# Division, bias, residual add and store moved from a stage of their own into the last third of the attention rows (graph network kernel, one core)

## The chip, the cores and the metric

The kernel runs on one core of one Trainium2 chip. The metric is the device time of one execution in microseconds (us), the lower the better. Three executions of the kernel before gave 4484.0, 4495.23 and 4496.08 us; the median is 4495.23 us.

## What is computed

Two message-passing layers on a graph of 12500 nodes (128 features) and 200000 edges, sorted by destination. The first layer ends in `x1` (the input plus its result). The second, an attention layer with 4 heads of 32 features, is where the change lies:

```
h = relu(layernorm(x1));  hW = (h @ W).reshape(N, 4, 32)
e = leaky_relu(a_src[src] + a_dst[dst], 0.2)         # edges and self loops
p = exp(e - segment_max(e, dst)[dst])
denom = segment_sum(p, dst)
out = segment_sum(hW[src] * p, dst) / (denom + 1e-16)   # per head
result = x1 + out + bias
```

The kernel sums numerator and denominator together and divides once at the end.

## The kernel before

Nodes lie in 98 windows of 128 nodes (a node is a partition), edges in 196 blocks of 1024. The attention pass walks 294 steps; each step handles one pair of an edge block and a window that meet, and passes on to the next block or window (196 + 98 = 294). Two steps make a row of the loop; the table `steps` in SBUF holds the block and window numbers of each row, and every engine loads its numbers from it at the row's start. In a row `u` is 0 in the first step and 1 in the second. The steps are software-pipelined: at step j the engines do the front of step j, the node part of j-1, the edge part of j-2 and the sum of j-3 or j-4. The order on each engine is that in which the code is written; semaphores join the engines.

The names that the change and the prediction touch:

- `a_G`: the rows of `Htab` for a block's edges, gathered by GpSimd (line 502) into 7 slots; SyncE tells VectorE (`ready`) that a block has landed.
- `a_Sb` (line 1354, VectorE): a one-hot matrix; ScalarE casts it to `a_S32` in two halves (line 1498), the second half when TensorE is done with the old one.
- `a_csh` (line 1358, VectorE), then `a_psD` (TensorE, line 1515), then `a_tt` (line 1394, VectorE).
- `a_ST` (line 1464, ScalarE): a copy of TensorE's transposes `a_psT`, and the first thing ScalarE does in a step.
- `a_GP` (line 1448, VectorE): the gathered rows times the edge weights, the last thing VectorE does in a step. TensorE sums it into `a_psA` (line 1525), 8 matrix products of float32, shown as 16.
- `acc`, shown as `arena` (128 partitions x window x 4 heads x 33): 32 sums and the denominator of each head. ScalarE scales it (line 1477), and VectorE adds `a_psA` to it (line 1350), the first thing VectorE does in a step.

VectorE loads the numbers of its row at line 1326, between `a_GP` of the row before and line 1350.

Window w gets its last sum at step 196 + w - 1 at the latest, so from step 197 on windows become final one after another.

After the attention pass a barrier closes its block of code. `final_phase` then works on 14 groups of 7 windows: SyncE loads `x1keep` into `f_x` (line 1582) and stores `f_o` to `out` (line 1587), GpSimd adds the bias (line 1606), VectorE forms the shares 1/(denominator + 1e-16) for all windows (lines 1613 and 1615), multiplies (line 1625, 7 instructions a group) and adds `f_x` (line 1634).

Of the kernel before, what the change touches and what calls it, by code (L numbers as in the profile page):

```python
# [25 lines left out]
P = 128  # L26
N, E = 12500, 200000
D, ED, H = 128, 64, 64
NH, HC = 4, 32
# [12 lines left out]
PIECE = 14  # L42
NG = W // GW
# [7 lines left out]
assert W == NG * GW and NG % 2 == 0 and NS % 2 == 0 and NB % SLOTS == 0  # L51

# [29 lines left out]
def build(nc, t, out):  # L82

    main = ExitStack()
    with main:
# [47 lines left out]
        with ExitStack() as ctx:  # L133
            attention_pass(nc, t, k, Htab, flagrows, lambda *a: sb(*a, ctx=ctx), sem, ctx)
        with ExitStack() as ctx:
            final_phase(nc, t, k, x1keep, out, lambda *a: sb(*a, ctx=ctx), sem, ctx)
# [45 lines left out]

def group(dram, g):

    return dram.rearrange("(g w p) f -> g p w f", w=GW, p=P)[bass.ds(g, 1)].rearrange("o p w f -> p (o w) f")
# [5 lines left out]


def run_groups(eng, body):


    body(0)
    with eng.Fori(1, NG // 2) as i:
        body(i)
# [271 lines left out]
def run_pairs(eng, body, count, depth, first=None):  # L470

    def edge(j, back):
        return 0 <= j - back < count
    for row in range(3):
        body(row, edge)
        if row == 0 and first is not None:
            first()
    with eng.Fori(3, count // 2 - 1) as row:  # L480
        body(row, lambda j, back: True)
    for row in range(count // 2 - 1, (count + depth + 1) // 2):
        body(row, edge)
# [764 lines left out]
def attention_pass(nc, t, k, Htab, flagrows, sb, sem, ctx):  # L1248
# [17 lines left out]
    GP = two("GP", [P, C, HR])  # L1266
    pst = lambda name, shape, dt=F32: ctx.enter_context(nc.psum_tensor(f"a_{name}", shape, dt))
# [6 lines left out]
             "h1 r1 h2 h3 EX eq es ed ep GP ACh ACC am ag").split()  # L1274
# [4 lines left out]
    with nc.Block() as block:  # L1279
# [12 lines left out]
        def _(dve):  # L1292
# [32 lines left out]
            def body(row, live):  # L1325
# [6 lines left out]
                for u in range(2):  # L1332
# [86 lines left out]
                    if node:  # L1419
# [31 lines left out]
            run_steps(dve, body, 4)  # L1451

        @block.scalar
        def _(act):
# [45 lines left out]
            run_steps(act, body, 3)  # L1500
# [67 lines left out]
def final_phase(nc, t, k, x1keep, out, sb, sem, ctx):  # L1568

    xs = [sb(f"f_x{u}", [P, GW, D]) for u in range(2)]  # L1570
    os_ = [sb(f"f_o{u}", [P, GW, D]) for u in range(2)]
    den = sb("f_den", [P, 2, W, NH])
    s_x = [sem(f"f_slotx{u}") for u in range(2)]
    s_st = [sem(f"f_stored{u}") for u in range(2)]
    s_v, s_xb, s_m, s_o = (sem(f"f_{n}") for n in ("v", "xb", "m", "o"))
    with nc.Block() as block:
        @block.sync
        def _(sp):
            def load(g, u, done):
                if due(done):  # L1580
                    sp.wait_ge(s_o, done)
                sp.dma_start(xs[u][:, :, :], group(x1keep, g)).then_inc(s_x[u], 16)  # L1582

            def store(g, u):
                if due(g + 1):
                    sp.wait_ge(s_o, g + 1)
                sp.dma_start(group(out, g), os_[u][:, :, :]).then_inc(s_st[u], 16)  # L1587

            for u in range(2):
                load(u, u, 0)  # L1590
            with sp.Fori(0, NG // 2 - 1) as i:
                for u in range(2):
                    load(2 * i + 2 + u, u, 2 * i + u + 1)
                    store(2 * i + u, u)
            for u in range(2):
                store(NG - 2 + u, u)
            for u in range(2):
                sp.wait_ge(s_st[u], 16 * (NG // 2))

        @block.gpsimd  # L1600
        def _(pool):
            def body(i):
                for u in range(2):
                    if due(16 * (i + 1)):
                        pool.wait_ge(s_x[u], 16 * (i + 1))
                    pool.tensor_tensor(xs[u][:, :, :], xs[u][:, :, :], bc(k["gbias"][:, :], 1, GW),
                                       ALU.add).then_inc(s_xb, 1)
            run_groups(pool, body)

        @block.vector  # L1610
        def _(dve):
            link = Count()
            dve.tensor_scalar(den[:, 0], k["acc"][:, 0:W, HC:HR:HC + 1], 1e-16, None, ALU.add).then_inc(s_v, 1)  # L1613
            dve.wait_ge(s_v, link())
            dve.reciprocal(den[:, 1], den[:, 0]).then_inc(s_v, 1)  # L1615
            dve.wait_ge(s_v, link())

            def body(i):
                for u in range(2):
                    g = 2 * i + u  # L1620
                    acc, share = k["acc"][:, bass.ds(g * GW, GW), :], den[:, 1, bass.ds(g * GW, GW), :]
                    if due(16 * i):
                        dve.wait_ge(s_st[u], 16 * i)
                    for w in range(GW):
                        ins = dve.tensor_tensor(  # L1625
                            os_[u][:, w, :].rearrange("p (h c) -> p h c", c=HC),
                            acc[:, w, 0:HR].rearrange("p (h c) -> p h c", c=HC + 1)[:, :, 0:HC],
                            bc(share[:, w, :], 2, HC), ALU.mult)
                    ins.then_inc(s_m, 1)
                    if due(g + 1):  # L1630
                        dve.wait_ge(s_m, g + 1)  # L1631
                    if due(g + 1):
                        dve.wait_ge(s_xb, g + 1)  # L1633
                    dve.tensor_tensor(os_[u][:, :, :], os_[u][:, :, :], xs[u][:, :, :], ALU.add).then_inc(s_o, 1)  # L1634
            run_groups(dve, body)


# [35 lines left out]
```

## Time and profile before

| | |
|---|---|
| median of three executions | 4495.23 us (4484.0 to 4496.08) |
| the profiled execution's own time | 4484.96 us |
| its span, first to last instruction | 4483.2 us |
| rows 100 to 145 of the attention pass | 3749.6 to 4377.6 us |
| rows 146 to 148 | 4377.6 to 4403.3 us |
| last stage | 4403.3 to 4483.2 us |
| busy share of the span: TensorE, its weight loads, VectorE, ScalarE, GpSimd | 86%, 78%, 54%, 60%, 72% |
| granted TensorE clock, mean | 0.80 of full speed |

Times in rows are microseconds from the span's start. A busy share is a mean over stages that differ, so the stages are read by themselves below. "Idle" is the time in which an engine ran no instruction, with the releaser that ended it; "issue" means that the profile shows nothing that it waited for.

### The profile page before, as it was taken

The page shows a single profiled execution, that of the slowest core. Times are in us where ns is not written, and L with a number is a line of the kernel's source. Part 1 is how long each engine was busy: PE and PEld are TensorE (multiplying, and loading weights), DVE is VectorE, ACT ScalarE, POOL GpSimd, SP SyncE. Part 2 cuts the span into 40 slices and gives each one's busy share as a digit, 9 for nine tenths or more (in the row PEclk, how much of TensorE's full clock was granted, in tenths as well). Part 3 has the DMA queues.
Part 4 walks back from the last instruction along what each step waited for, and adds up shares of the span by engine and source line. Part 5 has one row for each costly group of instructions (what it writes and reads, how often), then busy time and mean ns, then how long its engine had stood idle before and what let it go on. Part 6 is the DMA issues. An engine that isn't in the chain of part 4 may idle for free. (4 is left out here: it accounts for less than half of the span.)

```text
span 4483.2 us, 130400 instructions
## 1 busy us (share of the span) xinstructions
PE 3855.5 (86%) x40200; PEld 3479.7 (78%) x40201; DVE 2408.8 (54%) x9866; ACT 2697.7 (60%) x4960; POOL 3218.0 (72%) x3234
## 2 busy tenths in 40 slices
PE   6788888888888888887766999999999999999992
PEld 4677777777777777776456998889999899999992
DVE  5742222222222222222765777777777777777776
ACT  5555655565555655564554666666666666666661
POOL 2777777777777777775557777777777777777772
PEclk9898898989989899897776677777777766766765
DMA  5322222222222222221332222222222222222223
GB/s 159 78 54 52 52 52 54 50 54 52 52 52 52 52 52 52 52 52 44 100 109 56 55 56 55 54 55 55 55 55 55 55 55 55 56 55 55 56 53 115
DMA packets 288723, 272.91 MB, mean 61 GB/s; under 512 B 132751, under 2 KB 209829, under 8 KB 288677
## 3 DMA queue, kind: packets, MB, share of 16 engines
q0 software_dynamic: 100352, 160.76, 17.0%
q1 hardware_dynamic: 181392, 108.94, 8.6%
q10 hardware_dynamic: 6932, 2.69, 0.2%
q8 instruction: 17, 0.28, 0.0%
q14 instruction: 30, 0.24, 0.0%
HBM read 242.74 MB, written 29.40 MB: 61 GB/s over the span
## 5 line engine op out<-in xcount | busy, mean ns | idle before, releaser
L502 POOL DMA_INDIRECT a_G<-Htab,a_idx x1568 | 1526.9, 974 | 495.4 <-issue 474.7
L502 POOL DMA_INDIRECT p_rows<-Btab,p_idx x1568 | 1508.5, 962 | 478.9 <-issue 477.5
L1525 PE MATMUL a_psA<-a_GP,a_S 128*128 128x132 f32 x4704 | 949.8, 382 | 1.0 <-DVE a_GP L1448 1.0
L1525 PEld LDWEIGHTS a_psA<-a_GP,a_S 128*128 128x128 f32 x4704 | 871.7, 282 | 7.2 <-DVE a_GP L1448 1.3
L802 DVE TENSOR_TENSOR p_z<-p_psZ,p_rows 128x512 f32<-128x512 f32 x294 | 198.2, 689 | 1168.7 <-SPq L614 1124.3
L1498 ACT CAST a_S<-a_Sb 128x512 f32<-128x512 bf16 x588 | 635.5, 1126 | 75.5 <-PE a_psA L1525 74.0
L942 PE MATMUL p_psA<-p_msg,p_S 128*128 128x65 f32 x4704 | 619.1, 295 | 21.6 <-ACT p_S L880 21.6
L942 PEld LDWEIGHTS p_psA<-p_msg,p_S 128*128 128x128 f32 x4704 | 601.1, 211 | 25.1 <-issue 24.7
L875 ACT ACTIVATE p_msg<-p_z 128x512 f32<-128x512 f32 x294 | 182.2, 632 | 693.2 <-DVE p_z L802 668.6
L924 PEld LDWEIGHTS p_psZ<-wc,p_s 128*128 128x128 f32 x2352 | 339.6, 210 | 318.5 <-issue 312.4
L1464 ACT COPY a_ST<-a_psT 128x1024 bf16<-128x1024 bf16 x294 | 297.5, 1012 | 431.2 <-PE a_psT L1556 429.8
L880 ACT CAST p_S<-p_Sb 128x1024 f32 (+1 forms) x294 | 551.1, 1973 | 0.0
L924 PE MATMUL p_psZ<-wc,p_s 128*128 128x128 f32 x2352 | 348.0, 296 | 148.9 <-DVE p_z L802 148.8
L1551 PEld LDWEIGHTS a_psN<-a_R,a_Sb 128*128 128x128 bf16 x7056 | 472.6, 165 | 2.5 <-issue 0.2
L1551 PE MATMUL a_psN<-a_R,a_Sb 128*128 128x5 bf16 x7056 | 462.9, 200 | 0.0
L913 PE MATMUL p_psH<-arena,ew 128*128 x588 | 352.4, 684 | 98.8 <-issue 86.3
L862 ACT COPY p_ST<-p_psT 128x1024 bf16<-128x1024 bf16 x294 | 292.9, 1023 | 149.4 <-PE p_psZ L929 124.5
L1448 DVE TENSOR_TENSOR a_GP<-a_G,a_ep 128x1056 f32<-128x1056 f32 x294 | 367.2, 1249 | 0.7 <-ACT a_ep L1468 0.7
L902 PE MATMUL p_psT<-identb,p_Sb 128*128 128x128 bf16 x2352 | 272.2, 260 | 25.5 <-DVE p_Sb L834 19.7
L1539 PEld LDWEIGHTS a_psE<-nv,a_ST 128*128 128x128 bf16 x7056 | 236.6, 103 | 71.9 <-issue 59.1
L902 PEld LDWEIGHTS p_psT<-identb,p_Sb 128*128 (+1 forms) x2352 | 249.7, 151 | 44.8 <-issue 23.4
L1477 ACT ACTIVATE arena<-arena,a_f x1176 | 279.4, 311 | 3.4 <-DVE arena L1350 1.1
(220 smaller groups left out, 5245.4 us busy)
## 6 DMA issues: line engine op xcount, KB each, us to landing
arena<-in_ea SPq DMA_DIRECT2D x196, 256.0 KB
p_rows<-Btab,p_idx POOLq DMA_INDIRECT x1568
a_G<-Htab,a_idx POOLq DMA_INDIRECT x1568
Htab<-arena SPq DMA_DIRECT2D x14, 476.0 KB, 3.3
n_x<-in_x SPq DMA_DIRECT2D x14, 448.0 KB, 4.0
hTkeep<-n_hT SPq DMA_DIRECT2D x14, 448.0 KB, 3.1
u_hT<-hTkeep SPq DMA_DIRECT2D x14, 448.0 KB, 4.2
u_x<-in_x SPq DMA_DIRECT2D x14, 448.0 KB, 4.3
```

The costliest lines, as they stand in the source:

```text
L502: pool.indirect_dma_start(out=rows[:, u * C + c, :], out_offset=None, in_=table, in_offset=bass.IndirectOffsetOnAxis(ap=idx[u][:, c:c + 1] ...
L862: act.copy(ST[u][:, :, :], psT[u][:, :, :]).then_inc(s_ST, 1)
L880: act.copy(S32[u][:, :, :].rearrange("p c n -> p n c"), onehot(row - 3, u)).then_inc(s_S32, 1)
L902: m = pe.transpose(psT[u][:, c, :], hot[:, :, c], k["identb"][:, :])
L913: pe.matmul(psH[u][:, :], k["ew1"][:, :], ea[:, bass.ds(slot, 1), :].rearrange("p o e -> p (o e)"), start=True, stop=True).then_inc(s_H, 1)
L924: pe.matmul(psZ[u][:, 2 * e:2 * e + 2, :], s1[u][:, e * P:(e + 1) * P], k["wc2"][:, :], start=e == 0, stop=False)
L942: m = pe.matmul(psA[u][:, 0:H + 1], S32[u][:, c, :], msg[u][:, c, :], start=c == 0, stop=c == C - 1)
L1448: dve.tensor_tensor(GP[u][:, :, :].rearrange("p c (h f) -> p c h f", h=NH), G[:, slot2, 0:HR].rearrange("p c (h f) -> p c h f", h=NH), bc( ...
L1464: act.copy(ST[v][:, :, :], psT[:, :, :]).then_inc(s["ST"], 1)
L1498: m = act.copy(S32[v][:, cs, :].rearrange("p c n -> p n c"), Sb[v][:, :, cs])
L1525: m = pe.matmul(psA[v][:, 0:HR], S32[v][:, c, :], GP[v][:, c, :], start=c == 0, stop=c == C - 1)
L1551: m = pe.matmul(psN[:, 0:NH + 1], Sb[u][:, :, c], R[u][:, part, c, :], start=part == 0 and c == 0, stop=part == 2 and c == C - 1)
```

## The change

The last stage is gone, with its barrier, loads, stores and buffers. Its work is done two windows at a time in the rows 100 to 148 of the attention pass (q = row - 100, windows 2q and 2q+1). VectorE gets five more instructions in each of these 49 rows:

- `shares` (denominators + 1e-16, 128 x 8 elements), in the step u = 0 between `nq` and `ed`;
- `inverse` (reciprocal, 128 x 8), in u = 0 ahead of `make_ca`;
- `scaled` (numerators times shares into `a_part`, 128 x 256), in u = 1 behind the add to `acc` and ahead of `a_Sb`;
- `biased` (bias onto the loaded x1, 128 x 256), in u = 1 ahead of `a_tt`;
- `added` (`a_part` onto it, 128 x 256), in u = 1 ahead of `a_GP`.

ScalarE issues the transfers at the ends of its rows: the load of two windows of `x1keep` (128 KB) in rows 96 to 144, the store to `out` (128 KB) in rows 101 to 148, and one store behind the last row. The buffers `xo` are a ring of 8 in the memory of `agg`, which the attention pass does not use. `run_span` takes the place of `run_steps` on these two engines, so that rows with and without the new work have loops of their own: VectorE has a second loop from row 100 on, ScalarE writes rows 96 to 103 out and has further loops from rows 104 and 145 on.

```diff
+RX = 8
+LOAD, FIN, STORE = 96, 100, 101
...
+            def settled(row):
+                q = row - FIN
+                acc = k["acc"][:, bass.ds(2 * q, 2), 0:HR].rearrange("p w (h c) -> p w h c", c=HC + 1)
+                mine = xo[:, bass.ds(q % RX, 1)].rearrange("p o w f -> p (o w) f")
+
+                def shares():
+                    dve.wait_ge(s["ag"], 2 * row - 3)
+                    dve.tensor_scalar(share[:, 0], acc[:, :, :, HC], 1e-16, None, ALU.add).then_inc(s["den"], 1)
+
+                def inverse():
+                    dve.wait_ge(s["den"], 2 * q + 1)
+                    dve.reciprocal(share[:, 1], share[:, 0]).then_inc(s["den"], 1)
+
+                def scaled():
+                    dve.wait_ge(s["den"], 2 * q + 2)
+                    dve.tensor_tensor(part[:, :, :].rearrange("p w (h c) -> p w h c", c=HC), acc[:, :, :, 0:HC],
+                                      bc(share[:, 1], 3, HC), ALU.mult).then_inc(s["fm"], 1)
+
+                def biased():
+                    dve.wait_ge(s["xl"], 16 * (q + 1))
+                    dve.tensor_tensor(mine, mine, bc(k["gbias"][:, :], 1, 2), ALU.add).then_inc(s["fx"], 1)
+
+                def added():
+                    dve.wait_ge(s["fm"], q + 1)
+                    dve.wait_ge(s["fx"], q + 1)
+                    dve.tensor_tensor(mine, mine, part[:, :, :], ALU.add).then_inc(s["fin"], 1)
+                return shares, inverse, scaled, biased, added
...
+                    if done and u == 1:
+                        scaled()
...
+                    if done and u == 0:
+                        shares()
...
+                    if done and u == 1:
+                        biased()
...
+                    if done and u == 0:
+                        inverse()
...
+                    if done and u == 1:
+                        added()
...
-            run_steps(dve, body, 4)
...
+            run_span(dve, unsettled, 0, FIN)
+            run_span(dve, settling, FIN, FIN + W // 2)
...
+            def load_x1(q):
+                if due(q):
+                    act.wait_ge(s["xl"], 16 * q)
+                if due(q - RX + 1):
+                    act.wait_ge(s["out"], 16 * (q - RX + 1))
+                act.dma_start(xo[:, bass.ds(q % RX, 1)].rearrange("p o w f -> p (o w) f"), pair(x1keep, q)
+                              ).then_inc(s["xl"], 16)
+
+            def store_out(q):
+                act.wait_ge(s["fin"], q + 1)
+                if due(q):
+                    act.wait_ge(s["out"], 16 * q)
+                act.dma_start(pair(out, q), xo[:, bass.ds(q % RX, 1)].rearrange("p o w f -> p (o w) f")
+                              ).then_inc(s["out"], 16)
...
-def final_phase(nc, t, k, x1keep, out, sb, sem, ctx):
```

On VectorE, where the step u = 1 of a row begins (`arena` is `acc`; `ISA` and `REGISTER_ALU` are the sequencer's waits and address arithmetic), before:

```order
L1347 REGISTER_ALU
L1350 ISA
L1350 TENSOR_TENSOR arena<-arena,a_psA1 128x132
L1354 TENSOR_TENSOR a_Sb1<-iota_nc,a_rel1 128x1024
L1357 REGISTER_ALU
L1358 ISA
L1358 SCALAR_TENSOR_TENSOR a_csh1<-a_frow,a_psC 4x128
```

and in the changed kernel, rows 100 to 145:

```order
L1396 REGISTER_ALU
L1399 ISA
L1399 TENSOR_TENSOR arena<-arena,a_psA1 128x132
L1359 REGISTER_ALU
L1360 ISA
L1360 TENSOR_TENSOR a_part<-arena,a_share 128x256
L1405 TENSOR_TENSOR a_Sb1<-iota_nc,a_rel1 128x1024
L1408 REGISTER_ALU
L1409 ISA
L1409 SCALAR_TENSOR_TENSOR a_csh1<-a_frow,a_psC 4x128
```

The multiplication of two windows now stands between the add to `acc` and the one-hot matrix.

On VectorE at the end of a row, before:

```order
L1444 TENSOR_TENSOR a_R1<-a_r21,a_R1 128x40
L1448 ISA
L1448 TENSOR_TENSOR a_GP1<-a_G,a_ep 128x1056
L480 REGISTER_ALU
L480 COMPARE_AND_BRANCH
```

and in the changed kernel:

```order
L1501 TENSOR_TENSOR a_R1<-a_r21,a_R1 128x40
L1370 TENSOR_TENSOR agg<-agg,a_part 128x256
L1507 ISA
L1507 TENSOR_TENSOR a_GP1<-a_G,a_ep 128x1056
L497 REGISTER_ALU
L497 COMPARE_AND_BRANCH
```

The final add stands ahead of `a_GP`, and so ahead of the branch and the load of the next row's numbers.

On ScalarE at the end of a row, before:

```order
L1498 CAST a_S320<-a_Sb0 128x128x4 x2
L480 REGISTER_ALU
L480 COMPARE_AND_BRANCH
```

and in the changed kernel (rows 104 to 144):

```order
L1563 CAST a_S320<-a_Sb0 128x128x4 x2
L1568 ISA
L1570 ISA
L1571 ISA
L1571 DMA agg<-x1keep 128x2x128
L1575 REGISTER_ALU
L1577 ISA
L1578 ISA
L1578 DMA out<-agg 128x2x128
L497 REGISTER_ALU
L497 COMPARE_AND_BRANCH
```

Two issues of transfers, with their waits and addresses, now stand between the last cast of a row and the branch; behind the branch come the load of the row's numbers and the copy `a_ST`.

## Rows read from the trace of the kernel before

**Rows 1.** Windows: stretch, length, busy PE, PEld, DVE, ACT, POOL (instructions), clock, DMA share, GB/s

```profile
3749.60:4377.60 628.00, 603.08 (x6894) 576.22 (x6892) 477.78 (x2301) 419.25 (x1013) 468.67 (x484) 0.69 0.24 54
4377.60:4403.30 25.70, 24.02 (x268) 22.72 (x264) 16.78 (x70) 16.91 (x42) 0.00 (x0) 0.73 0.01 1
4403.30:4483.20 79.90, 0.00 (x0) 0.00 (x0) 56.67 (x114) 0.00 (x0) 29.45 (x14) 0.52 0.55 161
```

**Rows 2.** Waits, 3749.6 to 4377.6 us: who waited for whom, us in total, times, longest

```profile
ACT a_ST L1464 <- PE a_psT L1556: 139.7, 92, 2.0
DVE arena L1350 <- issue: 53.1, 39, 1.9
...
DVE a_Sb L1354 <- ACT a_S L1498: 30.1, 51, 0.7
...
DVE a_tt L1394 <- PE a_psD L1515: 20.5, 47, 0.8
DVE arena L1350 <- PE a_psA L1525: 16.4, 35, 0.7
...
PE a_psD L1515 <- DVE a_csh L1358: 14.1, 21, 1.7
PE a_psE L1539 <- DVE nv L1437: 9.4, 29, 0.5
```

**Rows 3.** Waits, 2417 to 3749.6 us, rows ahead of 100

```profile
DVE a_ca L68 <- SPq L532: 33.1, 36, 3.1
```

**Rows 4.** Timeline, 4100 to 4124 us: start, length, [idle before, releaser]

```profile
4101.75 2.07 PE L1525 MATMUL a_psA<-a_GP,a_S 128*128 128x132 f32 x16
...
4104.28 1.25 DVE L1448 TENSOR_TENSOR a_GP<-a_G,a_ep 128x1056 f32<-128x1056 f32 x1
...
4106.18 0.29 DVE L1350 TENSOR_TENSOR arena<-arena,a_psA 128x132 f32 x1 [0.64 <-issue]
...
4107.96 3.89 PE L1525 MATMUL a_psA<-a_GP,a_S 128*128 128x132 f32 x16
...
4111.89 1.13 ACT L1498 CAST a_S<-a_Sb 128x512 f32<-128x512 bf16 x1 [0.61 <-PE a_psA L1525]
...
4113.05 0.69 DVE L1354 TENSOR_TENSOR a_Sb<-iota_nc,a_rel 128x1024 bf16<-128x1024 bf16 x1 [0.69 <-ACT a_S L1498]
...
4114.45 0.22 DVE L1379 SCALAR_TENSOR_TENSOR a_nq<-a_psN,a_n,adst 128x4 f32<-128x4 f32 x1
4114.58 0.18 DVE L1384 TENSOR_TENSOR a_ed<-a_es,a_psE 128x32 f32<-128x32 f32 x1
...
4115.65 0.19 DVE L1394 TENSOR_TENSOR a_tt<-lead,a_psD 128x32 f32<-128x32 f32 x1 [0.79 <-PE a_psD L1515]
...
4117.77 1.25 DVE L1448 TENSOR_TENSOR a_GP<-a_G,a_ep 128x1056 f32<-128x1056 f32 x1
...
4120.89 0.29 DVE L1350 TENSOR_TENSOR arena<-arena,a_psA 128x132 f32 x1 [1.86 <-issue]
```

**Rows 5.** Timeline, 4402 to 4416 us: last add of the pass, last stage's first operations

```profile
4402.99 0.29 DVE L1350 TENSOR_TENSOR arena<-arena,a_psA 128x132 f32 x1 [1.99 <-PE a_psA L1525]
...
4404.17 2.60 DVE L1615 RECIPROCAL f_den<-f_den 128x392 f32<-128x392 f32 x1
...
4413.09 1.50 DVE L1625 TENSOR_TENSOR f_o<-arena,f_den 128x128 f32<-128x128 f32 x7
...
4414.62 1.09 DVE L1634 TENSOR_TENSOR f_o<-f_o,f_x 128x896 f32<-128x896 f32 x1
```

**Rows 6.** Line 350, issues of transfers on ScalarE's queue: min/median/max ns

```profile
L350 ACTq DMA_DIRECT2D ub<-in_upd_b x1: 473/473/473, 5.3 to 5.3; - x1
L350 ACTq DMA_DIRECT2D uw<-in_upd_b x1: 979/979/979, 5.8 to 5.8; - x1
```

**Rows 7.** Line 1587, stores of the last stage: issue ns, and us to landing

```profile
L1587 SPq DMA_DIRECT2D out<-f_o x14: 377/421/692, 4413.9 to 4479.7; - x14
...
DMA to landing us min/median/max: 3.0/4.8/5.3
```

More of the change, by code:

```diff
@@ L51 @@
 assert W == NG * GW and NG % 2 == 0 and NS % 2 == 0 and NB % SLOTS == 0
+assert W % 2 == 0 and 2 * FIN - 4 >= NB and FIN + W // 2 <= (NS + 5) // 2
 def due(n):
@@ L133, in build @@
         with ExitStack() as ctx:
-            attention_pass(nc, t, k, Htab, flagrows, lambda *a: sb(*a, ctx=ctx), sem, ctx)
-        with ExitStack() as ctx:
-            final_phase(nc, t, k, x1keep, out, lambda *a: sb(*a, ctx=ctx), sem, ctx)
+            attention_pass(nc, t, k, Htab, flagrows, x1keep, out, lambda *a: sb(*a, ctx=ctx), sem, ctx)
 def moments(dve, s_link, link, x, bn, mv, s_turn):
@@ L180, in split3, with pair @@
     dve.wait_ge(s_link, link())
+def pair(dram, q):
+    return dram.rearrange("(q w p) f -> q p w f", w=2, p=P)[bass.ds(q, 1)].rearrange("o p w f -> p (o w) f")
 def group(dram, g):
@@ L482, in run_pairs, with every, run_span, edge @@
     for row in range(count // 2 - 1, (count + depth + 1) // 2):
+        body(row, edge)
+def every(j, back):
+    return True
+def run_span(eng, body, lo, hi):
+    def edge(j, back):
+        return 0 <= j - back < NS
+    a, b = max(lo, 3), min(hi, NS // 2 - 1)
+    for row in range(lo, a):
+        body(row, edge)
+    if a < b:
+        with eng.Fori(a, b) as row:
+            body(row, every)
+    for row in range(max(a, b), hi):
         body(row, edge)
@@ L1266, in attention_pass @@
     GP = two("GP", [P, C, HR])
+    xo = k["agg"].rearrange("p w f -> p (w f)")[:, 0:RX * 2 * D].rearrange("p (r w f) -> p r w f", r=RX, w=2)
+    share = sb("a_share", [P, 2, 2, NH])
+    part = sb("a_part", [P, 2, D])
     pst = lambda name, shape, dt=F32: ctx.enter_context(nc.psum_tensor(f"a_{name}", shape, dt))
@@ L1273, in attention_pass @@
     names = ("ready turn init ca loc S T S32 ST TL csh TC tt ux Rf Rh r2 Rm Rl NM n1 nq nm mn f "
-             "h1 r1 h2 h3 EX eq es ed ep GP ACh ACC am ag").split()
+             "h1 r1 h2 h3 EX eq es ed ep GP ACh ACC am ag den fm fx xl fin out").split()
     s = {n: sem(f"a_{n}") for n in names}
@@ L1323, in _, with body @@
             make_loc(0, 0, first)
-            def body(row, live):
+            def settled(row):
[20 more added lines that the diff above has]
+                return shares, inverse, scaled, biased, added
+            def body(row, live, done=False):
+                shares, inverse, scaled, biased, added = settled(row) if done else (None,) * 5
                 v = nc.values_load_multi_w_load_instructions(
@@ L1450, in body, with unsettled, settling @@
                                           bc(ep[:, u, :, :], 3, HC + 1), ALU.mult).then_inc(s["GP"], 1)
-            run_steps(dve, body, 4)
+            def unsettled(row, live):
+                body(row, live)
+            def settling(row, live):
+                body(row, live, True)
+            run_span(dve, unsettled, 0, FIN)
+            run_span(dve, settling, FIN, FIN + W // 2)
         @block.scalar
@@ L1499, in body, with loading, moving, storing @@
                         m.then_inc(s["S32"], 1)
-            run_steps(act, body, 3)
+            def load_x1(q):
[11 more added lines that the diff above has]
+                              ).then_inc(s["out"], 16)
+            def loading(row, live):
+                body(row, live)
+                load_x1(row - LOAD)
+            def moving(row, live):
+                body(row, live)
+                load_x1(row - LOAD)
+                store_out(row - STORE)
+            def storing(row, live):
+                body(row, live)
+                store_out(row - STORE)
+            run_span(act, body, 0, LOAD)
+            for row in range(LOAD, LOAD + RX):
+                (loading if row < STORE else moving)(row, every)
+            run_span(act, moving, LOAD + RX, LOAD + W // 2)
+            run_span(act, storing, LOAD + W // 2, (NS + 4) // 2)
+            for q in range((NS + 4) // 2 - STORE, W // 2):
+                store_out(q)
+            act.wait_ge(s["out"], 16 * (W // 2))
         @block.tensor
@@ L1565, in _ @@
             run_steps(pe, body, 3)
-def final_phase(nc, t, k, x1keep, out, sb, sem, ctx):
[L1570 to L1635, printed above, removed]
```

6 lines of the change are left out of this document (1 added, 5 removed).

## The prediction

> **What bounds the kernel now.** I read the windows first, then the waits of one stretch, then one row of the timeline. The last stage takes the final 79.9 us of the span [rows 1]. TensorE does nothing there and VectorE is busy for 56.7 us of it; nothing of another stage runs beside it, so whatever it does elsewhere for less is won. Rows 100 to 145, where the work goes, take 628.0 us, which is 13.65 us for each of 46 rows. There TensorE is busy for 603.1 us (96%) at a granted clock of 0.69, VectorE for 477.8 us (76%), ScalarE for 67% [rows 1]. So VectorE is idle for 150.2 us, 3.27 us a row. How much of this can take work is the whole question.
>
> The waits split it. "issue" ahead of line 1350 is 53.1 us: the sequencer loading the row's numbers, 0.64 us in one row and 1.86 us in the next [rows 2, 4]. That stall lies behind `a_GP`, and work put ahead of `a_GP` doesn't use it. Room for work are the waits for others: 30.1 us for ScalarE's cast ahead of `a_Sb` (51 times), 20.5 us for `a_psD` ahead of `a_tt` (47 times), 16.4 us for `a_psA` ahead of line 1350 (35 times), 67.0 us or 1.46 us a row [rows 2]. The other way round, TensorE waits for VectorE 14.1 + 9.4 = 23.5 us, 0.51 us a row [rows 2]. So a row alternates between stretches that TensorE sets and stretches that VectorE sets.
>
> The timeline shows the loop that closes over a row. From one `a_GP` of u = 1 (4104.28) the path goes over the stall to line 1350 (4106.18), over `a_csh` and `a_psD` to `a_psA` (4107.96, 3.89 us), over ScalarE's second cast (1.13 us) to `a_Sb` of u = 1 (4113.05, idle 0.69), over `a_tt` (4115.65, idle 0.79) to the next `a_GP` (4117.77): 13.49 us [rows 4]. The gathers are not the limit in these rows: the wait for a landed block adds up to 33.1 us ahead of row 100 [rows 3], and none stands among the waits behind it.
>
> **What is removed.** The last add to `acc` starts at 4402.99 and ends at 4403.28 [rows 5]; from there to the span's end are 79.9 us. They shrink to a tail: `scaled`, `biased` and `added` of the last pair, one store, and the closing of the program. Size of the three: seven multiplications of 128 elements take 1.50 us, an add of 896 takes 1.09 us [rows 5]. Those rows give 1.06 ns for each further element and 0.20 us from one 128-element start to the next, so 256 elements cost 0.20 + 0.14 = 0.34 us, three of them 1.0 us, and 0.2 us for the hand-offs. The store: 3.0 us to landing is the quickest of 448 KB [rows 7]; 128 KB lies between a little and that, and I take 3.0 us whole because ScalarE's issue may be slower than SyncE's. Behind its landing the old program took 0.4 us to close (4479.7 + 3.0 to 4483.2). The tail is 4.6 us, and 75.3 us go.
>
> **What is added to a row.** VectorE gets three operations of 0.34 us, `shares` and `inverse`. Small operations follow each other in 0.13 us (4114.45 to 4114.58) [rows 4]; with address arithmetic I take 0.2 us for `shares`; `inverse` has 8 elements at 2.60 / 392 us [rows 5], 0.05 us, and 0.13 us. With 0.05 us for the two sequencer instructions ahead of `biased` the sum is 1.45 us a row: more busy time (71 us in 49 rows) than the old stage had on VectorE. Where each falls:
>
> - `shares`, `inverse` and `scaled`, 0.72 us, stand ahead of the wait for the cast (0.65 us a row if all of its 30.1 us falls to u = 1) and of that for `a_psA` (0.36 us a row) [rows 2]. The cast comes from TensorE's clock, not from VectorE, so the wait shrinks. Cost 0 to 0.1 us; without the cover 0.72.
> - `biased`, 0.39 us, stands right ahead of `a_tt`, whose wait is 0.22 us in the mean of 92 steps but uneven: where it is 0.79 us all is hidden, where TensorE is early nothing. Cost 0.15 us; bounds 0 and 0.39.
> - `added`, 0.34 us, stands in the loop ahead of `a_GP` with the stall behind it, and delays line 1350, `a_csh` and `a_psA` of the next row. Only a TensorE that is late there anyway takes it up. Cost 0.2 us; bounds 0 and 0.34.
> - ScalarE issues a load and a store at the row's end, each 0.47 to 0.98 us on its queue [rows 6], with waits and addresses. Queued behind them are the load of its numbers and the copy `a_ST`. Cover: the second cast (1.13 us) runs meanwhile, and ScalarE is idle 139.7 us for 92 copies, 1.52 us each [rows 4, 2]. Two issues of 0.6 us and 0.4 us of addresses are 1.6 us against 2.65 us. Cost nothing; without the cover 1.6 us a row.
> - The transfers add 256 KB in 13.65 us, 19 GB/s to 54 at a DMA share of 0.24 [rows 1]: nothing. Loads have four rows until `biased` needs them, and the stored pair was done in the row before. GpSimd and SyncE get nothing new.
>
> The sum is 0.4 us a row; 49 rows give 20 us, the three last rows included. A gain in the rows themselves has no reason, since nothing is taken from them.
>
> A loss through TensorE's clock has one. The granted clock is 0.69 in these rows: 38% of the time at 2.4 GHz and 62% at 1.2 GHz; the eight products of `a_psA` take 2.07 us in one place and 3.89 us in another [rows 1, 4]. Rows that are longer for the same products leave TensorE idler, and its clock may fall further. The Trainium skill ("TensorE: Matmul & The Clock Gate", Part 1: The HAM clock gate) says that the throttled clock is the default and activity releases it; by that this change loses more than its instructions cost. The rows don't settle it: the last stage, with TensorE idle, stands at 0.52 [rows 1], but no row shows what 0.4 us more a row does.
>
> **The sum.** 4484.96 (the profiled execution) - 75.3 + 20 = 4429.7 us. The median shown is 10.3 us above that execution, so the forecast for the median is 4440 us, a gain of 1.2%.
>
> **The rivals.** About 0.3%, 13.5 us, is what can be told from no change.
>
> 1. The rows don't grow. TensorE is busy for 96% of them, and all that VectorE adds (1.45 us) is about the room it has (1.46 us). Against it: `added` lies behind the waits, not ahead of them. Time 4495.2 - 75.3 = 4420 us. Chance 0.2.
> 2. Nearly all of VectorE's 1.45 us lies on the loop, because removing one of its waits only moves TensorE's. For it: TensorE already waits for VectorE 0.51 us a row. Growth 0.8 to 1.45 us, 39 to 71 us; times 4459 to 4491 us. Chance 0.15.
> 3. The clock falls. If half of the 2.4 GHz share goes (38% to 19%), each of two `a_psA` groups a row costs 0.19 x 1.82 us more, 0.69 us a row, 34 us in 49 rows, on top of the 20: 4474 us. Chance 0.08.
> 4. Slower than before: ScalarE's issues. If each takes the upper 0.98 us and the copies `a_ST` then come late in every row, `a_psE` and all behind it are late. Two issues and addresses are 2.4 us a row, 118 us, and 4495.2 - 75.3 + 118 = 4538 us. It decides against the change from 75.3 / 49 = 1.54 us a row, and is told apart from no change from 1.8 us. Against it is the 2.65 us of cover. Chance 0.07.
>
> **How the numbers follow.** The forecast (growth 0.15 to 0.8 us a row, 4427 to 4459 us) has 0.5. Faster by over 0.3% are it, rival 1, four fifths of rival 2 and rival 3's most: 0.5 + 0.2 + 0.12 + 0.05 = 0.87; I give 0.85. Within 0.3% (4482 to 4509 us) are the rest of 2 and 3: 0.08. Slower: 0.07. The range leaves out rival 4 and the upper end of 2 and 3: 4414 to 4480 us; the low end is rival 1 less half of the spread of the three executions shown.
>
> **What would show it.** The span ends about 5 us behind the last add to `acc`. Rows 100 to 145 take 645 us instead of 628. The wait ahead of `a_Sb` falls from 30.1 us to below 10, that ahead of `a_tt` by a third; ScalarE's wait ahead of `a_ST` shrinks but stays. `a_part` and the two writes to `agg` take 0.3 to 0.45 us each. Issues on ScalarE stay near 0.6 us. The prediction is wrong if those rows take 690 us or more, if TensorE's clock there is below 0.64, if the branches into the new loops stall for microseconds, or if waits for landed blocks come back behind row 100.

## The result, and the profile after

The changed kernel takes 4411.18 us (median of 4, 4408.61 to 4415.26) beside 4489.61 us for the kernel before on the same chip (median of 4, 4481.61 to 4496.08). The ratio is 0.9829, 95% interval 0.981 to 0.9848: 78 us faster, where 55 were forecast (4495.23 to 4440). The time lies 3 us below the range and 9 us below rival 1's 4420. The profiled execution took 4409.01 us, 75.95 less than that of before. Windows of the changed kernel (the columns of [rows 1]): rows 3 to 99, rows 100 to 145, the last three rows, and what is left behind the last add to `acc`.

```profile
2420.20:3748.40 1328.20, 1246.55 (x14550) 1192.90 (x14549) 1008.31 (x4851) 885.49 (x2135) 1010.97 (x1042) 0.72 0.25 56
3748.40:4378.30 629.90, 602.44 (x6902) 585.40 (x6902) 530.51 (x2530) 424.01 (x1013) 468.61 (x483) 0.75 0.32 73
4378.30:4403.80 25.50, 23.25 (x283) 22.25 (x282) 19.70 (x84) 17.15 (x42) 0.00 (x0) 0.86 0.08 22
4403.80:4407.20 3.40, 0.00 (x0) 0.00 (x0) 1.05 (x3) 0.00 (x0) 0.00 (x0) 0.85 0.13 39
```

Against [rows 1], the 79.9 us at the end became 3.4 (76.5 gone), rows 100 to 145 grew by 1.9, the last three rows lost 0.2, and what lies ahead of row 100 lost 1.2: 76.0 us, the whole difference. VectorE took up 52.7 us more work in rows 100 to 145 (477.8 to 530.5 us) in 1.9 us more time. The waits of this stretch show where it went, as in [rows 2]:

```profile
ACT a_ST L1529 <- PE a_psT L1656: 108.7, 72, 2.0
DVE arena L1399 <- issue: 48.2, 45, 1.9
...
ACT a_ST L1529 <- DMA agg<-x1keep: 30.0, 19, 1.6
...
PE a_psD L1615 <- DVE a_csh L1409: 22.1, 26, 2.1
...
DVE a_Sb L1405 <- ACT a_S L1563: 14.0, 40, 0.6
...
DVE a_tt L1449 <- PE a_psD L1615: 5.2, 17, 0.7
...
DVE arena L1399 <- PE a_psA L1625: 3.5, 13, 0.5
...
PE a_psE L1639 <- DVE nv L1494: 2.5, 7, 0.5
```

The three waits that the prediction called room for work fell from 67.0 us [rows 2] to 22.7, by 44.3 us beside 52.7 us added. Not all of that is the change's doing: in the kernel below that leaves the five operations out, the same three add up to 49.2 us. TensorE's two waits for VectorE stand at 24.6 us where they were 23.5: hardly more in sum, though the one for `a_csh` rose from 14.1 to 22.1 us. ScalarE's wait ahead of `a_ST` is 138.7 + 1.5 us in all, as before; a part of it now bears the name of the transfer that ScalarE issued just ahead. Waits for landed blocks stand at 22.6 us ahead of row 100, where [rows 3] have 33.1:

```profile
DVE a_ca L71 <- SPq L549: 22.6, 21, 4.2
```

VectorE's five new groups in rows 100 to 145 (busy us, mean ns of one | idle before them):

```profile
L1360 DVE TENSOR_TENSOR a_part<-arena,a_share 128x256 f32<-128x256 f32 x46 | 19.7, 427 | 0.0
L1365 DVE TENSOR_TENSOR agg<-agg,gbias 128x256 f32 x46 | 19.6, 425 | 5.6
...
L1370 DVE TENSOR_TENSOR agg<-agg,a_part 128x256 f32 x46 | 19.3, 419 | 0.0
...
L1356 DVE RECIPROCAL a_share<-a_share 128x8 f32<-128x8 f32 x46 | 9.1, 198 | 0.0
L1352 DVE TENSOR_SCALAR a_share<-arena 128x8 f32 x46 | 8.7, 189 | 0.0
```

ScalarE's two issues (min/median/max ns), which [rows 6] had bounded by 473 and 979, and the end of the program, where [rows 5] had the last stage begin:

```profile
L1571 ACTq DMA_DIRECT2D agg<-x1keep x49: 387/398/425, 3709.3 to 4365.7; - x49
```

```profile
L1578 ACTq DMA_DIRECT2D out<-agg x49: 387/397/483, 3778.4 to 4405.0; - x49
```

```profile
4403.46 0.29 DVE L1399 TENSOR_TENSOR arena<-arena,a_psA 128x132 f32 x1 [1.62 <-PE a_psA L1625]
4403.67 0.42 DVE L1360 TENSOR_TENSOR a_part<-arena,a_share 128x256 f32<-128x256 f32 x1
4404.01 0.42 DVE L1365 TENSOR_TENSOR agg<-agg,gbias 128x256 f32<-128x256 f32 x1
4404.53 0.43 DVE L1370 TENSOR_TENSOR agg<-agg,a_part 128x256 f32<-128x256 f32 x1
4404.99 0.39 ACTq L1578 DMA_DIRECT2D out<-agg  x1
```

From one start to the next are 0.34 us (4403.67 to 4404.01), as worked out for 256 elements. The program ends 2.2 us behind the last issue, where 3.4 had been taken.

In three of the five groups of runs below every kernel, the one before too, took 1.3 to 1.6 times as long (5923 to 7174 us, and one execution of the kernel before 8968 us); those runs are compared with each other only.

### The profile page after: what moved, and what is told of

It reads as the page before. It is cut to its first block and busy times, and to the rows that moved or that the text cites. A ratio compares the mean times of both kernels' runs of the same rounds, so it can differ in the third digit from the quotient of the medians.

```text
span 4407.2 us, 130927 instructions
## 1 busy us (share of the span) xinstructions
PE 3836.7 (87%) x40200; PEld 3470.6 (79%) x40201; DVE 2411.3 (55%) x9997; ACT 2700.6 (61%) x4960; POOL 3186.4 (72%) x3220
## 5 line engine op out<-in xcount | busy, mean ns | idle before, releaser
L1625 PE MATMUL a_psA<-a_GP,a_S 128*128 128x132 f32 x4704 | 959.9, 385 | 1.4 <-DVE a_GP L1507 1.4
L1625 PEld LDWEIGHTS a_psA<-a_GP,a_S 128*128 128x128 f32 x4704 | 884.7, 286 | 7.7 <-DVE a_GP L1507 1.7
L959 PE MATMUL p_psA<-p_msg,p_S 128*128 128x65 f32 x4704 | 607.3, 292 | 20.4 <-ACT p_S L897 20.3
L959 PEld LDWEIGHTS p_psA<-p_msg,p_S 128*128 128x128 f32 x4704 | 589.9, 207 | 23.5 <-issue 23.4
```

Of the source, the lines that this page charges most:

```text
L959: m = pe.matmul(psA[u][:, 0:H + 1], S32[u][:, c, :], msg[u][:, c, :], start=c == 0, stop=c == C - 1)
L1625: m = pe.matmul(psA[v][:, 0:HR], S32[v][:, c, :], GP[v][:, c, :], start=c == 0, stop=c == C - 1)
```

## The experiments

Two readings stood against each other from the start: rows 100 to 145 didn't grow because something else sets their pace (the gathers: GpSimd issues eight for each block, one start every 1.28 us in the mean, 196 blocks for 147 rows, 13.6 us a row, and it hardly ever waits for a free slot), or because the new operations fill VectorE's own waits. Growth is taken over the 46 rows 100 to 145.

How much such a stretch varies by itself can be read from rows 54 to 99, 46 rows that hold nothing of the change but the first four loads of `x1keep`. In the ten profiles at the normal pace (before twice, the changed kernel, and seven of the kernels below) they take 624.4 to 631.0 us, at a granted clock of 0.69 to 0.74. The shortest and the longest, half gathers and the kernel before:

```profile
3107.60:3732.00 624.40, 592.11 (x6902) 565.50 (x6902) 476.89 (x2301) 418.60 (x1013) 247.21 (x248) 0.72 0.13 29
```

```profile
3118.60:3749.60 631.00, 596.63 (x6926) 573.27 (x6925) 478.13 (x2301) 421.10 (x1013) 480.79 (x494) 0.73 0.24 55
```

So a difference of some 5 us between two single profiles says little. In the experiments that follow, the numbers of blocks and of uses on which engines wait are also masked by a register operation (`& 255`, `& 511`); the control has only that.

**Control, and the five operations left out.** The second kernel leaves the five VectorE operations out and stores what the load brought, so `out` is x1 alone; loads, stores and their issues stay.

```diff
-                    dve.wait_ge(s["ready"], b + 1)
+                    dve.wait_ge(s["ready"], (b & 255) + 1)
```

```diff
-                    if done and u == 1:
-                        scaled()
...
-                    if done and u == 1:
-                        added()
...
-                act.wait_ge(s["fin"], q + 1)
+                act.wait_ge(s["xl"], 16 * (q + 1))
```

> The changed kernel, with one more register operation (a bitwise and that changes no value) on the loaded numbers that engines wait against; the experiments below all carry it. Every theory: within 0.3% of the changed kernel (4398 to 4424 us), rows 100 to 145 in 627 to 633 us.

> The five VectorE operations of the settled rows are left out (the output is then x1 alone); loads and stores on ScalarE stay. Theory A, TensorE's alternating clock takes up what VectorE adds, and the row's length is held by the loop of TensorE and its clock: rows 100 to 145 in 627 to 632 us as with the operations, the granted clock there back from 0.75 to about 0.69, the waits of VectorE back to about 67 us. Theory B, the operations only fill idle time of VectorE: the same length, waits back, but no reason for the clock to move. Theory C, they do cost something (my forecast of 0.4 us a row): 610 us or less.

**More work on VectorE.** Two, or six, more additions of 256 elements into unused memory behind `added` and ahead of `a_GP`, in every row from 100 on.

```diff
+                    if due(q):
+                        dve.wait_ge(s["dump"], q)
+                    for r in range(2):
+                        m = dve.tensor_tensor(dump[:, r, :], part[:, :, :].rearrange("p w f -> p (w f)"),
+                                              part[:, :, :].rearrange("p w f -> p (w f)"), ALU.add)
```

> Two more additions of 256 elements into unused memory ahead of a_GP in every row from 100 on, 0.68 us a row. Theory A: the rows stay within 6 us of 630 us, or jump by a larger step once the rhythm no longer holds. Theory B: only the 0.49 us a row of waits that are left (22.7 us in 46 rows) can take work, and not all of it, so 640 to 661 us. A theory that gathers set the pace: like A here.

> Six more additions, 2.04 us a row, 94 us in 46 rows. All theories: longer rows, since VectorE is then busy or in its stall for over 14 us of a row. Theory B: 630 + 94 - 23 = 700 us. Theory A: 700 to 724 us, with the granted clock in these rows different from 0.75. My forecast's logic (all of it on the loop): 724 us.

Windows of rows 100 to 145 in the four kernels, in the order control, without the five, two more, six more:

```profile
3731.60:4369.70 638.10, 604.38 (x6899) 585.45 (x6897) 530.69 (x2531) 423.28 (x1013) 475.53 (x486) 0.73 0.30 72
```

```profile
3737.00:4368.10 631.10, 598.91 (x6898) 580.43 (x6898) 479.70 (x2301) 422.93 (x1013) 475.31 (x486) 0.75 0.31 73
```

```profile
3728.00:4373.90 645.90, 605.58 (x6881) 584.39 (x6879) 559.54 (x2621) 423.55 (x1013) 481.83 (x486) 0.72 0.30 71
```

```profile
3736.40:4412.00 675.60, 622.24 (x6913) 598.30 (x6910) 617.72 (x2801) 426.58 (x1013) 483.70 (x486) 0.67 0.29 68
```

The control took 4416.32 us (median of 4, 4400.09 to 4421.43) beside 4483.24 for before (median of 7): ratio 0.985, interval 0.9831 to 0.9869, 66.9 us faster where the changed kernel was 78.4. The other three were run once: 4397.66, 4405.49 and 4446.72 us. The five operations are 51.0 us of VectorE's time and cost 7.0 us in the rows (631.1 to 638.1). The next 28.9 us of work cost 7.8, the 58.2 us after them 29.7. A microsecond of work costs 0.14 and 0.27 us in the first two steps, which single profiles don't tell apart (with half gathers, below, it is 0.21 in both), and 0.51 in the third. So there is room on VectorE that fills up.

The rows of the control are longer than expected (638.1 us where 627 to 633 had been written). The kernel without the five fits none of its three theories: its rows are 7.0 us shorter than its twin's, where A and B had the same length and C 610 us or less, and the clock doesn't go back to 0.69. The one with two more falls in theory B's 640 to 661. For six more every theory had 700 us or more and the forecast's own logic 724; the rows took 675.6. Theory B had counted the waits for others, 23 us, as all the room there was. VectorE's waits in the control say which room (without the five operations, the second fence):

```profile
DVE arena L1399 <- issue: 50.5, 44, 2.1
DVE a_Sb L1405 <- ACT a_S L1563: 14.1, 44, 0.4
DVE a_tt L1449 <- PE a_psD L1615: 5.4, 16, 0.7
```

```profile
DVE arena L1399 <- issue: 63.6, 44, 2.2
DVE a_Sb L1403 <- ACT a_S L1553: 30.6, 47, 0.7
DVE a_tt L1443 <- PE a_psD L1605: 13.8, 55, 0.8
```

Of the 51.0 us, 38.0 went into the cast's wait (16.5 us), that for `a_psD` (8.4) and, against the prediction, the stall at the load of the row's numbers (13.1); the rows' growth is 7.0. The stall is the place of `added`, 0.34 us in 46 rows, 15.6 us. With two additions more the stall is 27.7 us, and with six 1.4:

```profile
DVE arena L1406 <- issue: 27.7, 24, 1.4
```

```profile
DVE arena L1406 <- issue: 1.4, 4, 0.8
```

One row shows how; the timeline of the control, and then that of six more, `added` first:

```profile
4102.98 0.42 DVE L1370 TENSOR_TENSOR agg<-agg,a_part 128x256 f32 x1
4103.31 1.25 DVE L1507 TENSOR_TENSOR a_GP<-a_G,a_ep 128x1056 f32<-128x1056 f32 x1
4106.27 0.29 DVE L1399 TENSOR_TENSOR arena<-arena,a_psA 128x132 f32 x1 [1.71 <-issue]
```

```profile
4101.64 0.42 DVE L1371 TENSOR_TENSOR agg<-agg,a_part 128x256 f32 x1
4101.97 2.09 DVE L1375 TENSOR_TENSOR agg<-a_part 128x256 f32<-128x256 f32 x6
4103.98 1.25 DVE L1514 TENSOR_TENSOR a_GP<-a_G,a_ep 128x1056 f32<-128x1056 f32 x1
4105.18 0.29 DVE L1406 TENSOR_TENSOR arena<-arena,a_psA 128x132 f32 x1
```

The additions stand ahead of `a_GP`, the load behind it in the program, and yet the stall is gone. The records fit one reading: the sequencer had handed the additions and `a_GP` over and gone on to the load while they ran. By the load's own records in the traces it starts 0.50 us behind the start of `a_GP` in the kernel before, 0.23 us behind it in the control, 0.36 us ahead of it with two additions more and 1.5 us ahead with six (means of rows 100 to 145). Already in the kernel before, the load ran beside `a_GP`, not behind it.

**The gathers' pace.** From its second filling on, each slot is filled with four of its eight groups of 128 records; the other half keeps old ones, so attention's results are not the reference's. This kernel ran as it is, without the five operations, and with two additions more, beside the kernel before.

```diff
-        for c in range(C):
+        for c in range(C if used is None else few):
...
-            sp.wait_ge(s_g[u], 16 * C * (i + 1 + turns))
+            sp.wait_ge(s_g[u], 16 * (C // 2) * i + 16 * C * (1 + turns))
...
-            gather_blocks(nc, pool, Htab, G, idx, s["GP"], s["turn"], k, NB // SLOTS)
+            gather_blocks(nc, pool, Htab, G, idx, s["GP"], s["turn"], k, NB // SLOTS, few=C // 2)
```

> Every block that is gathered anew in the attention pass brings four of its eight groups of 128 records; the other half of the slot keeps old records. All else is as in the changed kernel. Theory A (the gathers' pace is the floor of these rows): the rows 10 to 99, 13.66 us each in the control, fall below 13.2 us, and rows 100 to 145 below 638 us by at least 10 us. Theory B (the engines' own chain sets the rows and hid the five operations): rows 10 to 99 stay within 0.1 us of 13.6 us, and rows 100 to 145 stay at 630 to 640 us.

> Half gathers as in the run before it, and the five VectorE operations of a row (shares, inverse, scaled, bias, sum) left out; the store waits on the load of x1 instead. Theory A (the operations were hidden under the gathers' pace): with that floor gone their price shows, so rows 100 to 145 are shorter here than with them by 0.3 us a row or more, 14 us or more in all. Theory B (they lie in VectorE's own idle waits): the same within 5 us.

> Half gathers, and two more additions of 256 elements (0.34 us each) in every row from 100 on, ahead of the release of a block. Theory A (a row has no slack on the engines): rows 100 to 145 are 20 to 31 us longer than with half gathers alone. Theory B (VectorE's idle takes them): longer by 0 to 8 us.

> The kernel before, whole, as the mate of the three others on the same chip. Both theories: 4485 us within 15, rows 100 to 145 628 us within 10.

They took 4401.4, 4392.72, 4420.98 and 4470.88 us, each run once. GpSimd's waits in rows 100 to 145 show the gathers' pace gone (the control first, then half gathers):

```profile
POOL a_G L519 <- issue: 148.1, 486, 0.3
```

```profile
POOL a_G L519 <- DVE a_GP L1507: 318.0, 57, 10.1
```

GpSimd now waits 318 us for free slots, and the rows don't mind: rows 10 to 99 take 13.61 us each with half gathers (1225.3 us in 90 rows), 13.64 in the kernel before of this group and 13.66 in the control. Windows of rows 100 to 145, with the five operations, without, two more, and the kernel before:

```profile
3732.10:4372.10 640.00, 606.65 (x6900) 587.35 (x6899) 529.42 (x2531) 423.72 (x1013) 224.86 (x228) 0.73 0.18 44
```

```profile
3734.20:4363.10 628.90, 602.80 (x6885) 585.52 (x6882) 477.07 (x2301) 425.03 (x1013) 216.06 (x228) 0.75 0.18 45
```

```profile
3743.50:4389.50 646.00, 606.89 (x6879) 586.35 (x6876) 557.05 (x2621) 424.17 (x1013) 221.00 (x228) 0.72 0.18 44
```

```profile
3738.30:4363.80 625.50, 591.00 (x6917) 566.65 (x6916) 477.00 (x2301) 418.21 (x1013) 470.51 (x486) 0.73 0.24 55
```

The reading by the gathers falls: without their pace the row is as long as with it. The five operations cost 11.1 us here (0.24 us a row) and 7.0 with full gathers, the two additions 6.0 and 7.8. The expectation had put 14 us or more under the gathers' reading and at most 5 under the other; 11.1 lies between, and it is the 318 us of GpSimd's waits with rows of 13.61 us that decide. The rest came as theory B had it: rows 10 to 99 at 13.6 us, rows 100 to 145 at 640.0, the two additions at 6.0 us of 0 to 8; and the kernel before lies within what both had for it. VectorE's stall at the load goes the same way as before, 60.7 us without the five operations, 52.5 with them and 28.7 with two additions more:

```profile
DVE arena L1399 <- issue: 60.7, 41, 2.3
```

```profile
DVE arena L1399 <- issue: 52.5, 43, 2.0
```

```profile
DVE arena L1406 <- issue: 28.7, 24, 1.4
```

That the gathers don't hold these rows doesn't make them slack. All eight of a block take 13.6 us a row, which is where the engines stand too, so a shorter chain of the engines would meet them; this is argued, since no run at this pace has one.

**Three groups at another pace.** One kernel has rows of 12 numbers in the table of steps, of which it reads the first 10 as before; the others combine that with half gathers, or repeat kernels above.

```diff
-            ("steps", [1, NS // 2 + 2, 2 * NV], I32),
+            ("steps", [1, NS // 2 + 2, 2 * NV + 2], I32),
```

> The rows of the table of block and window numbers are 12 numbers long instead of 10, so that each begins at a multiple of 16 bytes; every other load of a row's numbers on VectorE took 2.29 us instead of 1.07, and I take that for the address. If so, all loads take 1.07 us and the stall at a row's start is 0.65 us in every row. Theory A (the rows are held by TensorE and its alternating clock): rows 100 to 145 within 4 us of 631 us. Theory of VectorE's loop: 0.6 us a row shorter, 603 us. Theory C, gathers hold the pass: rows 10 to 99 stay at 13.65 us each whatever VectorE does, and the whole kernel gains less than 10 us.

> GpSimd issues four of a block's eight gathers from the second turn of the slots on, so half of a_G is old data (the output is wrong); everything else is as in the control. Theory C, the gathers' pace of 10.2 us a block, 13.6 us a row, holds the pass: rows 10 to 99 fall from 1229 us to below 1200, and so do rows 100 to 145 from 630 to 638 us to below 620. Theory A or B: the rows from 100 on stay at 628 to 638 us, and of the rows ahead of 100 only the waits for landed blocks go (up to 33 us in 1332).

> Both: half the gathers and the table in rows of 12 numbers (the output is wrong). The engines' own pace with the shorter stall. If VectorE's loop sets it, rows fall by 0.6 us each against the half gathers alone, to 13.0 us or less; if TensorE's clock holds them, no change.

> The kernel before, with the same added register operation as the control, for a second look at its rows. If the granted clock in rows 100 to 145 is a property of the kernel, it is 0.69 again, against 0.75 with the changed rows; if it is chance, it is anywhere between. Rows 100 to 145 in 626 to 638 us, as long as with the five operations.

> The kernel of e3_aligned (table rows of 12 numbers) again; in the job of the first attempt every kernel, the one before too, took 1.6 times as long, with gathers landing late. Theory C, gathers hold the pass: the whole is within 10 us of the control (4400 to 4420 us) although each second row loses 1.2 us of stall. If VectorE's loop holds the rows from 100 on: those 46 rows 603 us and the whole 4385 us or less.

> The kernel of e4_half_gather (four gathers of a block's eight; output wrong) again. It takes GpSimd's pace away (5.1 us a block in place of 10.2). Theory C: rows fall below 13.4 us, with the five operations and without. Theory A or B: rows from 100 on stay at 13.65 to 13.9 us, only waits for landed blocks ahead of row 100 go.

> Half the gathers and none of the five VectorE operations (output wrong): against e4b_half_gather it gives what the five operations cost the engines' own loop in 46 rows, with the gathers out of the way. Theory C (the gathers hid the cost): e4b's rows are longer than these by my 0.4 us a row or more, 18 to 67 us in all. Theory B (VectorE has the room): less than 5 us.

> The kernel before with the control's register operation, again. Rows 100 to 145 in 626 to 638 us; granted clock there 0.69 if it belongs to the kernel, up to 0.75 if it is chance.

> The changed kernel with rows of 12 numbers in the table of block numbers instead of 10, of which it still reads 10: all loads of VectorE then take 1.07 us, where every second one took 2.29 us, 0.61 us less in a row. Theory A (the engines' own chain and the pace of the gathers both stand at 13.6 us a row, and either alone holds the time): rows 10 to 99 stay within 0.1 us of 13.65 us each, the time within 12 us of 4411 us. Theory B (the engines' chain alone sets a row): a row loses 0.2 to 0.6 us, the time is 4330 to 4385 us. Theory C (VectorE's load lies in time in which VectorE is waited for by nobody): rows as in theory A, and in the run after this one too.

> The same table with rows of 12 numbers, and half gathers (four of a block's eight groups of 128 records). Theory A: with both limits moved, rows 10 to 99 fall to 13.0 to 13.4 us each. Theory B: as in the run before it, 13.0 to 13.4 us in both. Theory C: 13.6 us a row in both.

| group | kernel | us | us a row, 10 to 99 | rows 100 to 145, us |
|---|---|---|---|---|
| 1 | 12 numbers | 7077.19 | 23.96 | 1042.2 |
| 1 | half gathers | 5988.62 | 16.14 | 740.0 |
| 1 | half gathers, 12 numbers | 5978.05 | 16.03 | 737.0 |
| 1 | before | 7150.33 | 24.17 | 1038.0 |
| 2 | 12 numbers | 6991.6 | 23.85 | 1051.0 |
| 2 | half gathers | 5923.06 | 15.93 | 735.3 |
| 2 | half gathers, without the five | 5926.86 | 15.86 | 736.8 |
| 2 | before | 7075.69 | 23.62 | 1059.0 |
| 3 | 12 numbers | 7062.22 | 23.80 | 1062.8 |
| 3 | half gathers, 12 numbers | 6002.6 | 16.15 | 734.2 |

The expectations were written for the normal pace, so only the one on the loads (1.07 us each, see the last section) can be judged by these runs; it came true. The kernel with 12 numbers against the one before of its group (medians 7134.45, 7055.93 and 7153.06 us) has ratios 0.9926 (0.9902 to 0.9949), 0.9916 (0.9878 to 0.9954) and 0.986 (0.9825 to 0.9894). Here the number of gathers does matter, 24 us a row against 16, which is not so at the normal pace; it isn't GpSimd's issuing that holds them, for in the kernel before of group 1 GpSimd waits for free slots for 964.1 of the 2200 us from 3800 to 6000. With half gathers, the shorter loads are worth 0.11 us a row in one pair (16.14 to 16.03), less than the 0.21 between two runs of the same kernel (16.14 and 15.93), and the five operations show nothing (735.3 and 736.8). The profile names "remote" or "issue" for most of the added idle time, and what slows a whole group isn't known. No run at the normal pace has the table of 12 numbers, so whether it makes the changed kernel faster stays open. A hint that it may: in rows 100 to 145 of the kernel before, rows with the long load take 13.97 us in the mean and the others 13.33, and every profile at the normal pace has such a difference. Against it stands the gathers' 13.6 us. No kernel here is shown to be faster than the changed one.

## Why the prediction was wrong, point by point

- **What is removed: right, a little small.** The tail was put at 4.6 us and is 3.4. The three operations and the hand-offs are 1.2 us, as worked out; the store from issue to the end takes 2.2 us instead of 3.4. 76.5 us went, where the forecast had 75.3. (What the old program took to close behind the last landing is 4483.2 - 4482.7 = 0.5 us, not 0.4, and the 1.06 ns for each further element needs the 0.28 us that one 128-element multiplication took, which isn't among the rows shown. Neither moves the sum by more than 0.1 us.)
- **The sum of 0.4 us a row: the step that failed.** It gave 18.4 us in rows 100 to 145. They grew by 1.9 us in the profiled pair; the control stands 10.1 and 12.6 us above the two profiles of before (628.0 and 625.5), 7.0 above its twin without the operations, and 11.1 is the price with half gathers. All together the growth is 0.04 to 0.27 us a row, below 0.4 everywhere; the twins give 0.15 and 0.24, about half of what was forecast. The changed kernel and its control, all but the same program, are 8 us apart (629.9 and 638.1), so it can't be had more finely from single profiles.
- **`added` at 0.2 us: the term at fault.** The prediction said "That stall lies behind `a_GP`, and work put ahead of `a_GP` doesn't use it". The runs show that it does: between the twins the stall falls by 13.1 us, and by 8.2 with half gathers, for the 15.6 us of `added`; by 22.8 more for two further additions, to 1.4 us for six. Two additions in the same place, 28.9 us of work, cost 7.8 and 6.0 us; at that price `added` costs 3 to 4 us, some 0.08 us a row instead of 0.2 (an estimate, since no run leaves out `added` alone). The stall, 53.1 us or 1.15 us a row, belonged to the room beside the 1.46 us. The Trainium skill says, in "Vector Engine (DVE) Microarchitecture Reference", 1.3 What the handler produces, that what the handler makes of an instruction is pushed onto a hardware FIFO which the engine drains; the load's start ahead of `a_GP` (0.36 and 1.5 us) agrees with that.
- **`shares`, `inverse`, `scaled` at 0 to 0.1 us, `biased` at 0.15 us: not told apart.** The cast's wait fell from 30.6 to 14.1 us between the twins, 16.5 us for the 37.5 us of the first three, so it took up a good part; it had been expected below 10 us. The wait ahead of `a_tt` fell by 8.4 us of the 15.6 that `biased` brings. The 7.2 us that are left are 0.16 us a row, as forecast, but they would be all of the twins' growth. It had been expected to fall by a third and fell by more than half. No run leaves out one of the four alone.
- **ScalarE's issues: little or nothing, and wrong in size.** 0.40 us each, not 0.6; rival 4 had 0.98. No run leaves them out alone; the two kernels with them and without the five operations (631.1 and 628.9 us) stand 1 to 6 us above the profiles of before, within what the rows vary by. ScalarE's wait ahead of `a_ST` didn't shrink in sum (139.7 to 140.2 us); the prediction had said that it would.
- **The transfers: right.** 73 GB/s instead of 54 at a share of 0.32, and the waits that bear their name (30.0 and 1.5 us ahead of `a_ST`) leave ScalarE's sum as it was.
- **"The gathers are not the limit in these rows": right**, as half gathers with rows of 13.61 us show, but the reason given was weak. The second profile of before has 17.8 us of waits for landed blocks in rows 100 to 145, where the first has none, and its rows are the shortest of all (625.5 us).
- **The clock (rival 3): not in this kernel, and only hinted at elsewhere.** The granted clock was 0.69 in the profile of before, 0.73 in its second profile (with the control's register operation) and 0.75 in the changed kernel's; the sign of being wrong was to be 0.64. Among twins it goes down with VectorE's work: 0.75, 0.73, 0.72, 0.67 for none, five, two and six more, and 0.75, 0.73, 0.72 again with half gathers. TensorE's idle time goes up from 32 us to 53 in the first four. Only the 0.67, at 3.0 us of added work a row, lies outside the 0.69 to 0.74 of rows 54 to 99. The Trainium skill's "TensorE: Matmul & The Clock Gate", Part 1: The HAM clock gate, makes activity what releases the clock; those four rows agree, and the two profiles of before don't (0.69 with 24.9 us idle, 0.73 with 34.5).
- **The rivals.** Rival 1, with chance 0.2, is nearest: the profiled pair has its rows, while the twins lie between it and the forecast. Its reason, room that about equals the work, holds with the load's stall as more room. Rival 2 (0.8 to 1.45 us a row) falls: even the five and six additions together cost 44.5 us in 46 rows, 0.97 us a row for 3 us of work.
- **The 28.8 us** between forecast and measurement: 18.3 are growth that did not come in the profiled pair, 1.2 the tail, 1.2 the rows ahead of 100, and 8.1 the step from a profiled execution to a median, 10.3 us for before and 2.2 for the changed kernel. Part of this is chance. The control, the same program but for the register operation, was 66.9 us faster than the kernel before of its group; taken from 4495.23 that is 4428 us, inside the range. So the mechanism was wrong in one term, and that the time fell outside the range took luck besides.

What stays open: what makes up the 13.61 us of a row once gathers and VectorE's room are out. The waits point to the alternation of TensorE and VectorE over `a_csh`, `a_psD` and `a_psA`, but no run shortened either. Open, too, is what the rows would be with a shorter chain, since the gathers' own 13.6 us stand beside it.

## What to carry to other kernels

When work is put on an engine that isn't the bound, look for room in each idle gap beside it, on both sides of the instruction: a stall of the sequencer (a load of registers) is room for work that stands ahead of it in the program, as long as the sequencer can hand that work over and go on. An end stage on which nothing else runs is the safest thing to fold in, since it is gone whole while the price in the rows is a part of the work. A producer that never pauses is no proof that it sets the pace; halve its work and see whether the rows move. And before a few microseconds between two profiles are explained, look at how much a stretch varies that the change doesn't touch.

## What the runs showed of the hardware

VectorE's load of 10 numbers into registers takes 1.07 us in one row and 2.29 in the next, all through the attention pass. With table rows of 12 numbers (48 bytes in place of 40), of which 10 are read, the loads of both kinds of row take 1.07 us. The control (10 numbers), whose median of 1683 ns lies halfway between the two kinds, and the kernel with 12:

```profile
L1375 DVEq TENSOR_LOAD <-steps x46: 1062/1683/2634, 3731.3 to 4355.8; - x46
```

```profile
L1375 DVEq TENSOR_LOAD <-steps x149: 365/1066/1310, 3560.2 to 7057.1; - x149
```

The second line comes from the first of the three groups at another pace, but the kernel before of that group, with 10 numbers, has loads of 1.07 and 2.29 us in turn, too (medians of the even and the odd rows). So the length hangs on where the row starts. Rows of 40 bytes start 0 and 8 bytes off a multiple of 16 in turn, if the table itself starts on one, and rows of 48 bytes never off it. Other distances weren't tried. The Trainium skill ("DMA: Bandwidth & Descriptors", Latency and other measured facts) gives such a load a floor of about 600 ns and says nothing of the address. Here VectorE's loads of two numbers from the same table take 530 ns (line 580 of the changed kernel, 441 loads), so the floor doesn't hold for them.
